# A recommender tower on one core: the plain fp32 group of layer 1 becomes a split group, and GpSimd computes one group's low parts

## The reference, cut to what matters

```
e   = stack(tbl_f[ids[:, f]] for f in range(39))        # (512, 39, 16)
z0  = einsum('bid,bjd->bdij', e, e)                      # layer 0: all pairs
cur0 = relu(einsum('bdk,kl->bld', z0, W0))               # 128 channels
h, direct0 = split(cur0, 2, axis=1)                      # 64 and 64
z1  = einsum('bid,bjd->bdij', e, h)                      # layer 1: 39 x 64 products
cur1 = relu(einsum('bdk,kl->bld', z1, W1))               # 128 channels
z   = sum(concat([direct0, cur1], axis=1), axis=-1)      # (512, 192)
y   = relu(relu(concat([z, dense]) @ W_top1 + b1) @ W_top2 + b2) @ W_top3
```

## Time and profile before

| | |
|---|---|
| median of 3 runs | 482.69 us (482.2 to 483.02) |
| profiled execution | 482.86 us |
| its span, first to last instruction | 480.7 us |
| mean granted clock of TensorE | 0.979 |
| busy PE / DVE / ACT / POOL | 434.3 / 350.1 / 227.4 / 247.9 us |

### The profile page before, as it was taken

How to read it: one execution, slowest core, us unless ns; L and a number is a source line. 1 busy time by engine, 2 the same in 40 slices (tenths; PEclk the granted TensorE clock), 3 DMA queues, 4 the chain that set the end, 5 groups by cost and what they waited for, 6 DMA issues and landing times.

```text
span 480.7 us, 4397 instructions
## 1 busy us (share of the span) xinstructions
PE 434.3 (90%) x1618; PEld 244.7 (51%) x1618; DVE 350.1 (73%) x197; ACT 227.4 (47%) x218; POOL 247.9 (52%) x180
## 2 busy tenths in 40 slices
PE   0244699999999999999999999999999999998798
PEld 0211265565656564646555556555565656564453
DVE  0300567988988888888888889797988988887900
ACT  3011633737464645554545546363737464643303
POOL 5877788888888585858585858677000000000000
PEclk9998599999999999999999999999999999998999
DMA  8212010101010100101010101010101010000000
GB/s 295 73 33 39 13 36 4 40 7 40 5 29 17 27 17 16 28 15 26 12 31 5 38 5 40 4 38 6 35 0 37 0 36 1 0 1 1 0 0 2
DMA packets 15563, 12.61 MB, mean 26 GB/s; under 512 B 6352, under 2 KB 12629, under 8 KB 15414
## 3 DMA queue, kind: packets, MB, share of 16 engines
q1 hardware_dynamic: 9204, 9.14, 6.7%
q0 software_dynamic: 5632, 1.35, 3.4%
q10 hardware_dynamic: 706, 1.84, 1.1%
HBM read 9.74 MB, written 2.56 MB: 26 GB/s over the span
## 4 chain that ended last, share of the span: by engine, by line
PE 88%; DMA 4%; DVE 3%; SPq 1%; issue 1%; ACT 1%; ACTq 0%; DVEq 0%
PE acc L418 23%; PE acc L448 12%; PE acc L440 12%; PE acc L441 12%; PE acc L456 11%; PE spread L429 7%; PE sums L408 6%; DMA mix_sb<-in_mix_dram 3%; PE sums L509 1%; DVE z L340 1%; DVE z_lo L348 1%; DMA x_parts<-x_rows 1%; PE spread L502 1%; PE spread L500 1%; SPq L193 1%
## 5 line engine op out<-in xcount | busy, mean ns | idle before, releaser
L233 POOL DMA_INDIRECT found<-in_table_dram,rows_sb x176 | 247.7, 1408 | 86.6 <-issue 51.2
L340 DVE TENSOR_TENSOR z<-spread,h 128x2048 f32<-128x2048 f32 x80 | 183.2, 2290 | 71.3 <-PE spread L429 55.8
L348 DVE TENSOR_TENSOR z_lo<-z,z_hi 128x2048 fp32r<-128x2048 f32 x64 | 146.2, 2284 | 0.0
L276 ACT ACTIVATE z_hi<-z 128x2048 fp32r<-128x2048 f32 x64 | 122.5, 1913 | 41.2 <-DVE z L340 41.2
L418 PE MATMUL acc<-squares,w 128*128 128x512 f32 x224 | 116.6, 638 | 0.0
L440 PE MATMUL acc<-z_hi,w_hi 128*128 128x512 f32 x256 | 103.0, 402 | 2.1 <-ACT z_hi L276 2.1
L441 PE MATMUL acc<-z_hi,w_lo 128*128 128x512 f32 x256 | 101.2, 395 | 0.0
L448 PE MATMUL acc<-z_lo,w_hi 128*128 128x512 f32 x256 | 90.5, 475 | 3.9 <-DVE z_lo L348 3.9
L252 ACT ACTIVATE squares<-sums 128x1024 f32<-128x1024 f32 x64 | 58.7, 917 | 48.6 <-PE sums L408 48.3
L448 PEld LDWEIGHTS acc<-z_lo,w_hi 128*128 128x128 f32 x256 | 47.2, 190 | 36.5 <-issue 22.0
L440 PEld LDWEIGHTS acc<-z_hi,w_hi 128*128 128x128 f32 x256 | 48.6, 190 | 21.9 <-issue 11.2
(11 more groups left out here) (30 smaller groups left out, 93.7 us busy)
## 6 DMA issues: line engine op xcount, KB each, us to landing
x_parts<-x_rows SPq DMA_DIRECT2D x64, 64.0 KB, 2.2
found<-in_table_dram,rows_sb POOLq DMA_INDIRECT x176, 2.4
w_sb<-in_w_dram SPq DMA_DIRECT2D x1, 1280.0 KB, 6.8
x_rows<-found_hi SPq DMA_DIRECT2D x32, 26.8 KB
x_rows<-found_lo SPq DMA_DIRECT2D x32, 26.8 KB
z<-in_select_dram ACTq DMA_DIRECT2D x1, 768.0 KB, 7.6
wt_sb<-in_wt_dram SPq DMA_DIRECT2D x1, 512.0 KB
w<-in_w0a_dram ACTq DMA_DIRECT2D x1, 448.0 KB, 9.7
```

What stands on the lines that cost most here:

```text
L233: pool.indirect_dma_start(out=found[:, b, s * D:s * D + D], out_offset=None, in_=table, in_offset=bass.IndirectOffsetOnAxis(ap=rows_sb[:, ...
L276: nc.scalar.activation(z_hi[:, n % RING], z[:, n % RING], ACT.Copy).then_inc(hi_done, 1)
L340: nc.vector.tensor_tensor(z[:, n % RING], spread[:, :, :], h[:, c % 2, :].unsqueeze(1).to_broadcast([P, QUADS, N]), ALU.mult).then_inc(mul ...
L348: nc.vector.tensor_tensor(z_lo[:, n % RING], z[:, n % RING], z_hi[:, n % RING], ALU.subtract).then_inc(lo_done, 1)
```

## The change

Group 4 becomes a split group like the others: `w1_hi` and `w1_lo` cover all 20 tiles, `high_part(n)` and `contract1_hi(n)` run for every n, and `contract1_whole` is gone. The low part of group 1 (`POOL_G`) moves from DVE to POOL, which computes it in four quarters of 512 columns and counts them in `pool_lo_done`. POOL gathers four chunks first, and then, for each chunk c, computes the low part of group 1 and gathers chunk c + 4. `BUFS` is 4. On PE the low part of group 4 stands in the next chunk's group 0, directly behind its spread; that of group 1 stands one group later than before, in group 3, in front of that of group 2.

```diff
-VT = (G - 1) * QUADS
-VG = G - 1
+POOL_G = 1
 RING = 3
 RING0 = 2
-BUFS = 3
+BUFS = 4
...
-        w1_hi = sb("w1_hi", [P, VT, P], F32R)
-        w1_lo = sb("w1_lo", [P, VT, P], F32R)
+        w1_hi = sb("w1_hi", [P, T1, P], F32R)
+        w1_lo = sb("w1_lo", [P, T1, P], F32R)
...
+        def wait_lo(engine, n):
+
+            if on_pool(n):
+                engine.wait_ge(pool_lo_done, QUADS * pool_count(n))
+            else:
+                engine.wait_ge(lo_done, vector_count(n))
...
+            def low_part(n):
+                pool.wait_ge(hi_done, n + 1)
+                if n >= RING:
+                    pool.wait_ge(contracted1, n - RING + 1)
+                for a in range(QUADS):
+                    nc.gpsimd.tensor_tensor(z_lo[:, n % RING, a], z[:, n % RING, a], z_hi[:, n % RING, a],
+                                            ALU.subtract).then_inc(pool_lo_done, 1)
+
+            pool.wait_ge(rows_ready, 1)
+            for c in range(BUFS):
+                gather(c)
+            for c in range(CHUNKS):
+                low_part(G * c + POOL_G)
+                if c + BUFS < CHUNKS:
+                    gather(c + BUFS)
...
-                    if is_v(n):
-                        high_part(n)
+                    high_part(n)
...
-                    if is_v(n):
+                    if not on_pool(n):
                         low_part(n)
...
+                    if n and g == 0:
+                        contract1_lo(n - 1)
                     if c + 1 < CHUNKS and g < ND:
                         if ND * (c + 1) + g + 1 < ND * CHUNKS:
                             add_up(ND * (c + 1) + g + 1)
                         contract0(ND * (c + 1) + g)
-                    if n and is_v(n - 1):
+
+                    if g and on_pool(n - 2):
+                        contract1_lo(n - 2)
+                    if g and not on_pool(n - 1):
                         contract1_lo(n - 1)
-                    if is_v(n):
-                        contract1_hi(n)
-                    else:
-                        contract1_whole(n)
+                    contract1_hi(n)
+            contract1_lo(G * CHUNKS - 1)
```

More of the change, by code:

```diff
@@ L46, with on_pool, pool_count, vector_count @@
 SPREAD_FROM = [0, 20, 10, 30]
-VT = (G - 1) * QUADS
-VG = G - 1
+POOL_G = 1
 RING = 3
 RING0 = 2
-BUFS = 3
[L55 to L61, removed]
+BUFS = 4
+def on_pool(n):
+    return n % G == POOL_G
+def pool_count(n):
+    return n // G + (n % G >= POOL_G)
+def vector_count(n):
+    return n + 1 - pool_count(n)
 def pairs():
@@ L164, in build @@
         lo_done = sem("lo_done")
+        pool_lo_done = sem("pool_lo_done")
         contracted1_hi = sem("contracted1_hi")
@@ L225, in _, with gather @@
         def _(pool):
-            pool.wait_ge(rows_ready, 1)
-            for c in range(CHUNKS):
+            def gather(c):
                 b = c % BUFS
@@ L272, in high_part @@
                 act.wait_ge(multiplied, n + 1)
-                if n >= RING and is_v(n - RING):
-                    act.wait_ge(lo_done, v_count(n - RING))
-                    act.wait_ge(contracted1_hi, v_count(n - RING))
+                if n >= RING:
+                    wait_lo(act, n - RING)
+                    act.wait_ge(contracted1_hi, n - RING + 1)
                 nc.scalar.activation(z_hi[:, n % RING], z[:, n % RING], ACT.Copy).then_inc(hi_done, 1)
@@ L286, in _ @@
             act.wait_ge(w1_in, 16)
-            nc.scalar.activation(w1_hi[:, :, :], w1_sb[:, 0:VT, :], ACT.Copy).then_inc(w1_hi_ready, 1)
+            nc.scalar.activation(w1_hi[:, :, :], w1_sb[:, :, :], ACT.Copy).then_inc(w1_hi_ready, 1)
             split(0)
@@ L335, in multiply @@
                 dve.wait_ge(spread_done, n + 1)
[L336 to L339, removed]
+                if n >= RING:
+                    wait_lo(dve, n - RING)
                 nc.vector.tensor_tensor(z[:, n % RING], spread[:, :, :],
@@ L344, in low_part @@
             def low_part(n):
-                dve.wait_ge(hi_done, v_count(n))
-                if n >= RING and is_v(n - RING):
+                dve.wait_ge(hi_done, n + 1)
+                if n >= RING:
                     dve.wait_ge(contracted1, n - RING + 1)
@@ L373, in _ @@
             dve.wait_ge(w1_hi_ready, 1)
-            nc.vector.tensor_tensor(w1_lo[:, :, :], w1_sb[:, 0:VT, :], w1_hi[:, :, :],
+            nc.vector.tensor_tensor(w1_lo[:, :, :], w1_sb[:, :, :], w1_hi[:, :, :],
                                     ALU.subtract).then_inc(w1_lo_ready, 1)
@@ L436, in contract1_hi @@
                     pe.wait_ge(evicted1, c)
-                pe.wait_ge(hi_done, v_count(n))
+                pe.wait_ge(hi_done, n + 1)
                 for a in range(QUADS):
@@ L445, in contract1_lo @@
                 g, r = n % G, n % RING
-                pe.wait_ge(lo_done, v_count(n))
+                wait_lo(pe, n)
                 for a in range(QUADS):
                     last = nc.tensor.matmul(acc1[:, :], w1_hi[:, QUADS * g + a, :], z_lo[:, r, a, :],
[L449 to L457, removed]
+                                            start=False, stop=(g == G - 1 and a == QUADS - 1))
                 last.then_inc(contracted1, 1)
```

## The result

| | before | after |
|---|---|---|
| median, same chip | 482.86 us (482.2 to 483.28, 4 runs) | 499.18 us (498.98 to 499.65, 4 runs) |
| profiled execution; its span | 482.86; 480.7 us | 499.09; 497.2 us |
| mean granted clock of TensorE | 0.979 | 0.979 |
| chunk, group 4 to group 4, in mid-run | 25.24 us | 26.49 us |

The change is slower: ratio 1.0342, 95% interval 1.0327 to 1.0356. Lines of the changed kernel: `spread_out` L452, `add_up` L431, `contract0` L441, high part L463 and L464, low part L471, multiply L363, DVE's low part L371, `evict1` L295, `z_hi` L302, POOL's gathers L243 and quarters L253.

What follows compares the result with a forecast made beforehand. PE, with its queue full throughout, was taken to bound the kernel. 482.86 + 0.6 (start) + 17.4 (14 boundaries) - 0.7 (end) = 500.2, against a forecast median of 500.0 us; range 492 to 508.

Steps and rivals of the forecast that it cites:

- the boundary: From group 4's spread to the next chunk's second spread: predicted 1.24 us dearer than before, at 14 boundaries.
- S: Zero of the predicted boundary times: the start of group 4's `spread_out` on PE.
- first wait (z_lo): PE reaches low(4) at 3.94 but its data from DVE allow 5.13: a wait of 1.19 us.
- n0: The next chunk's group 0, whose spread, z_hi and high part follow group 4 at the boundary.
- POOL's quarters start; one quarter: POOL's low(1) starts 11.7 us after S, about 1.2 us a quarter, 5 us in all, hidden within 9.6 us of room.
- Middle: +17.4 predicted: Mid-run chunks grow from 25.24 to 26.48 us, at 14 boundaries with a full chunk behind them: +17.4 us.
- one chain: At the boundary multiply, low(4) on DVE, its matmuls, evict1, z_hi(n0) and high(n0) follow one another; 9.67 us becomes 10.91.
- The second wait, 0.52: PE, free at 8.36, waits until 8.88 for z_hi(n0), which stands behind evict1 on ACT: about 0.52 us.
- Start: +0.6 predicted: DVE's w1_lo grows by a quarter, 0.57 us, delaying found_lo of chunk 0, x and all of PE.
- End: -0.7 predicted: From chunk 14's group 4 to the first MLP matmul, before 29.95 us: POOL takes one subtract off DVE, -0.7.
- the bounds: Limits given for the end term: 0 and -2.2 us, the latter with no clock dip.
- GpSimd becomes the limit, or blocks DVE: Rival: POOL quarters and DVE low parts delay each other, deciding above 1.9 us a quarter; 516 us at 2.28; chance 0.08.

Runs made afterwards that it cites:

- x2: The change with the next chunk's `add_up` put in front of low(4) on PE; 499.58 us, ratio 1.0361.
- x5: The change with the low part of group 1 given back to DVE, so POOL only gathers; 501.20 us, ratio 1.0390.
- x8: The change with high(n0) before evict1 on ACT, `add_up` before low(4) on PE, and group 1's low part back on DVE; 483.04 us, ratio 1.0014.
- x1: The change with group 0's z_hi put in front of the previous chunk's evict1 on ACT; 504.25 us, ratio 1.0446.
- x3: The change with both z_hi(n0) before evict1 on ACT and `add_up` before low(4) on PE; 501.26 us, ratio 1.0396.
- x10: x9 with the low part of group 1 on POOL again; 485.18 us, ratio 1.0053.
- x9: x8 with one step of layer 0 moved from group 3 into group 4; 473.80 us, ratio 0.9819.
- x13: x3 with each POOL quarter waiting until the one before it is through; 505.58 us, ratio 1.0474.
- x6: The change with every POOL quarter computed twice, the second waiting for the first; 568.68 us, ratio 1.1782.

## Why the prediction was right

500.0 was predicted, 499.18 measured. The step that carries it, the boundary:

| after S, us | predicted | measured |
|---|---|---|
| PE starts low(4) | 5.13 | 5.15 |
| first wait (z_lo) | 1.19 | 1.26 |
| evict1 | 6.34 | 6.39 |
| z_hi(n0) | 6.84 | 6.89 |
| high(n0) | 8.88 | 8.93 |
| next spread | 10.91 | 10.95 |
| chunk | 26.48 | 26.49 |
| POOL's quarters start; one quarter | 11.7; 1.2 | 11.83; 1.29 |

- **Middle: +17.4 predicted.** From group 4 of chunk 0 to that of chunk 14 (78.36 to 448.97) 370.61 us, before 352.89: +17.72. That it is one chain was argued; x2, x5 and x8 showed it. x4 has the fourth buffer and low(1)'s new place without the split group, and its chunk is 25.2 as before, so these two cost nothing there.
- **The second wait, 0.52, was mis-sized.** `contract0` starts at 217.58 and in mid-chunk the next matmul comes 1.42 after it (222.67 to 224.09), so PE was free at 219.00 and waited 0.79; the row's 0.23 counts from a modelled end. I had taken the work between as 2.2 us, in which a wait of before, about 0.34, was hidden; the work is 0.44 + 1.42 = 1.86. The sum goes by the chain, so nothing came of it.
- **Start: +0.6 predicted, -0.25 measured.** DVE's w1_lo took 2.80 instead of 2.27 and the first sums came 0.29 later (30.25 after 29.96), but group 4 of chunk 0 came at 78.36 instead of 78.61: the first spread is 0.28 later (30.97 after 30.69), the second already 0.13 earlier (55.19 after 55.32). Only the 0.53 of w1_lo can be read from this. Up to the second spread x1, x2 and x3 run the same instructions as the change, and there that spread starts at 55.23, 53.67 and 56.77: the start differs by 3 us from one execution to another, so one profile of each does not tell +0.6 from -0.25.
- **End: -0.7 predicted, -0.98 measured**, with the clock fall, as the bounds had it. The steps agree less than the sum: the spread of group 1 came 12.34 us after group 4's (461.31), not 11.5, since high(n0) took 3.41 in place of 2.61 while the clock was down, and the next group made it up with 3.36 in place of 4.29. In x2, whose last chunk is that of the change, the granted clock fell to 0.50 (456 to 459 us) and this stretch took 30.13, so the size of this term is good to about 1 us. x4 shows that POOL's part is worth about 3 us there; the split of group 4 takes 2 of them back.
- Together -0.25 + 17.72 - 0.98 = 16.49; 482.86 + 16.49 = 499.35, and 0.27 less around the span is the profiled 499.09. The +17.4 was worked out step by step; that the misses of start and end (-0.85, -0.28) and that of the middle (+0.32) cancel in part is luck.
- **The rival "GpSimd becomes the limit, or blocks DVE"** did not come in the change, but it was near: POOL waited 1.96 us in a chunk of 26.49. Its own chunk was 24.5, not the 23.7 that I worked out, and the 1.2 us a quarter was a choice between two bounds that no row made. The condition that I gave the rival, over 1.9 us a quarter, was wrong: x1 came over the edge at 1.29 a quarter with a boundary only 0.45 us shorter, and x3 with one 1.09 shorter. What I had not seen is that POOL's chunk depends on where its gathers meet DVE's subtractions: 22.8 in x4, 24.5 in the change, 26.0 in x10, 27.3 in x3, with the same instructions on POOL. My expectations for x1 and x3 failed by it; that the change stayed clear of it was in part luck.

## What to carry to other kernels

Cheaper matmuls that need one more step on another engine can cost more than they save: follow the chain of the new operand to the next matmul that must wait, and count the work that covers it. Shortening the chain brought the time back to that of before (x8), and independent work moved into the gap on top of it brought the gain (x9); moving the work alone was not tried. An engine that is idle for 2 us in a period can become the bound by a gain elsewhere, so its period is to be worked out for the faster kernel too.

## What the runs showed of the hardware that was not expected

- Four quarters on POOL that follow each other without a wait keep a subtraction on DVE with both inputs in SBUF out until the last is through: in x3 the low part begun at 202.21 ended at 207.66, 2.16 after POOL's quarters (205.50), about its own length; in x1 and x10 it ended 2.16 after them too. With a wait between the quarters DVE got in after one (x13: 3.10; x6: 3.28), and POOL paid (one quarter 3.31). The Trainium skill, "SBUF — State Buffer", Summary: rules for kernel authors, says of such pairs that the second one to issue is blocked until the first is through. x13 and x6 agree; x3 shows more, for there it lasted until the fourth instruction was through.
- A gather issued while such a subtraction runs takes 1.9 to 2.9 us, mostly over 2.7, instead of 1.0 (38 gathers in the change, such as the one at 230.50, and 37 in x3), and 3.6 where the split of found_lo and a low part follow each other (x3, 218.94). The 79 gathers that the change issues during a multiply, whose input `spread` lies in PSUM, took 0.99 to 1.01. The section Who interferes with whom of the Trainium skill, "SBUF — State Buffer", infers that this kind of DVE instruction does not stall such transfers; these rows say that it does, and the rows decide.
- A quarter on POOL took 1.287 us, all four 5.02, against 2.28 on DVE for the same columns.
